# An attention LSTM in a decoder: wait order, place of an output gate product, sums, alphas and cell order inside one time step

## The chip, the cores and the metric

The kernel runs on one core of a Trainium2 chip, in float32. The metric is the device time of one execution in microseconds. The median of three executions of the kernel before is 5745.92 us (5745.6 to 5747.82). A stretch of 512 dependent time steps of an LSTM with attention takes most of it.

## The reference, cut to what matters

The program is a two-layer decoder over x of shape (4, 512, 256). All five edits lie in the second block of the first layer, an LSTM (hidden size 256) whose input at each step contains the attention output of the step before. For a batch of 4 and 512 steps, in short:

```
for t in range(512):
    gates = x[t] @ W_x + attn @ W_attn + h @ W_hid + b      # i, f, g, o: 1024 columns
    c = sigmoid(f) * c + sigmoid(i) * tanh(g)
    h = sigmoid(o) * tanh(c)
    alpha = softmax((h @ Wq) . context)                      # over 512 source positions
    attn = tanh([alpha @ context, h] @ Wout)
    x[t] += attn
```

Each step needs the one before it whole, so its latency counts 512 times.

## The kernel before, in words

Everything of the step lies on chip. The keys already hold Wq and the values already hold the context part of Wout. Sigmoids are computed as tanh of half the argument. TensorE's array is used as four quarters (QUARTERS = 4): a product such as `gate_sums`, `scores` or `context` is issued as instructions to the four quarters that run side by side, and a float32 matmul appears in the trace as two weight loads and two matmuls. So one call of `scores(c, k)`, `context(c, n)`, `half_attn(c, k)` or `half_hid(c, k)` is eight loads and eight matmuls.

The hidden state, the cell and the gates i, f, g are kept in two halves k = 0, 1 of the hidden units. `gates` (L892 on) computes the next step's gates: `o_gate_x_hid` (the o gate's x part and both hidden parts, 64 columns each), `half_attn` four times (96 columns each; it waits for `attn_ready[0]` and before its second call for `attn_ready[1]`), then `o_gate_attn`. VectorE transposes each half (`turn_half`, L1011), ScalarE takes its tanh (L978) and the o gate's (L982, between the two halves), VectorE makes the products and the new cell (`cell_products` L1016, `new_cell` L1022), transposes the o gate (L1046), ScalarE takes tanh of the cell (L986), and `new_hidden` (L1029) gives half of h. TensorE multiplies h with the keys: `scores(c, k)` for four source chunks c; with half 0 of h chunks 0 and 1 can start, and then `h_ready[1]` is needed.

The softmax is done in two parts of two chunks each: VectorE takes the negated maximum (L1053), ScalarE the exponential (L989), TensorE turns the result with `turn(part)` (L882), and it is copied to `alpha` (part 0 on ScalarE, L993; part 1 on VectorE, L1063). `context(c, n)` (L873) adds chunk c into three column pieces n of 128, 64 and 64. Beside it VectorE and ScalarE work out the scale of the parts (`lstm_shrink` L995, `lstm_own_terms` L1068, ... `lstm_sel_scaled` L1080), the three pieces are copied to `out_row` (L998, L1000 on ScalarE, L1083 on VectorE), `select(o)` (L890) forms the attention row and ScalarE's tanh (L1004) gives `attn`. GpSimd adds it to x (L1097) and signals `attn_kept`.

Every engine runs its list in the order written; what sets the order is that list and the `wait_ge` calls in it. The DMA queue of SyncE loads one row of x parts a step (L795); no edit touches it.

The lines touched: L840 to L847 (o gate), L939 to L947 (turn and context), L986 to L1004 (ScalarE), L1047 to L1067 (VectorE).

Of the kernel before, what the change touches and what calls it, by code (L numbers as in the profile page):

```python
# [17 lines left out]
KC = DIM // P  # L18
# [644 lines left out]
def attention_lstm_phase(nc, d, g):  # L663
# [14 lines left out]
    with Scope(nc) as s:  # L678
# [14 lines left out]
        with Scope(nc) as q:  # L693
# [57 lines left out]
            first_total_ready = q.sem("lstm_first_total_ready")  # L751
# [33 lines left out]
            def alpha_rows(part):  # L785
                return alpha[:, :, 2 * part:2 * part + 2, SPACE - 1]
# [22 lines left out]
            def _(pe):  # L809
# [3 lines left out]
                def gate_sums(ps, cols, rows, w, start=False, stop=False):  # L813

                    for j in range(QUARTERS):
                        mm = pe.matmul(ps[j * STRIP:j * STRIP + ROWS, :], rows, w[:, j * HID + cols.start:j * HID + cols.stop],  # L816
                                       start=start, stop=stop)
                    return mm
# [17 lines left out]

                def o_gate_x_hid(u):

                    gate_sums(o_gate_ps, o_cols, place, xg[:, u, :], start=True).then_inc(xg_used, 1)
                    for c in range(KC):  # L840
                        gate_sums(o_gate_ps, o_cols, hid[:, c, PAD:PAD + ROWS], w_hid[:, c, :])

                def o_gate_attn():

                    for c in range(KC):
                        mm = gate_sums(o_gate_ps, o_cols, attn[:, c, 0:ROWS], w_attn[:, c, :], stop=c == KC - 1)
                    mm.then_inc(o_ready, 1)  # L847
# [70 lines left out]
                with pe.Fori(0, SEQ // UNROLL) as i:  # L918
                    for u in range(UNROLL):
# [17 lines left out]
                        for n in range(PIECES):  # L937
                            context(0, n)
                        pe.wait_ge(exp_ready, 2 * t + 2)  # L939
                        turn(1)  # L940
                        for n in range(PIECES):
                            context(1, n)
# [22 lines left out]
            def _(act):  # L965
# [4 lines left out]
                with act.Fori(0, SEQ // UNROLL) as i:  # L970
                    for u in range(UNROLL):
# [15 lines left out]
                        for part in range(PARTS):  # L987
                            act.wait_ge(max_ready, 2 * t + part + 1)
                            act.activation(expo[:, part, :], score_ps[part], ACT.Exp, bias=neg_max[:, part:part + 1],  # L989
                                           accum_out=total[:, 1:PARTS] if part == 1 else None).then_inc(exp_ready, 1)  # L990
                            if part == 0:
                                act.wait_ge(alpha_turned, 2 * t + 1)
                                act.copy(alpha_rows(0), turned_rows(0)).then_inc(alpha_ready[0], 1)  # L993
# [7 lines left out]
                        act.wait_ge(attn_kept, t + 1)  # L1001
                        for o in range(KC):
                            act.wait_ge(attn_summed[o], t + 1)
                            act.activation(by_batch(attn[:, o, :]), attn_ps[o], ACT.Tanh).then_inc(attn_ready[o], 1)  # L1004

            @block.vector
            def _(dve):
# [30 lines left out]
                with dve.Fori(0, SEQ // UNROLL) as i:  # L1038
                    for u in range(UNROLL):
# [7 lines left out]
                        cell_products(t, 1)  # L1047
                        new_hidden(t, 0)
                        new_cell(t, 1)
# [10 lines left out]
                        dve.wait_ge(exp_ready, 2 * t + 1)  # L1060
                        dve.tensor_reduce(total[:, 0:1], expo[:, 0, :], AX_X, ALU.add).then_inc(first_total_ready, 1)
                        dve.wait_ge(alpha_turned, 2 * t + 2)
                        dve.tensor_copy(alpha_rows(1), turned_rows(1)).then_inc(alpha_ready[1], 1)  # L1063
                        dve.wait_ge(first_total_ready, t + 1)
                        dve.wait_ge(exp_ready, 2 * t + 2)
                        dve.transpose(spread_blocks(spread_total[:, :]), every_row(total[:, :])).then_inc(total_spread, 1)
# [1578 lines left out]
```

## Time and profile before

| | us |
|---|---|
| median of the three runs | 5745.92 |
| the profiled execution's own time | 5744.19 |
| its span in the profile | 5742.4 |
| first to last tanh wait of the 512 steps (511 periods) | 195.4 to 3934.0 |

Outside this loop lie the preparation (the first 190 us) and the second half of the decoder (after 3934 us), which the change leaves alone. The trace gives instructions with start and length in us on each engine; PE is TensorE's matmuls, PEld its weight loads, DVE VectorE, ACT ScalarE, POOL GpSimd; a row with xN merges N neighbouring instructions, with its length from the first start to the last end. In brackets stands the idle time of the engine before it and what ended it.

### The profile page before, as it was taken

Reading aid. Unit: us, or ns where it says so; the run is one execution under the profiler, and the core shown is the slowest. Engines: PE = TensorE matmul, PEld = TensorE weight load, DVE = VectorE, ACT = ScalarE, POOL = GpSimd, SP = SyncE. Lnnn points to the kernel's source line nnn. Section 1 sums busy time; section 2 is a strip of 40 time slices with the busy share of each in tenths; the row PEclk is TensorE's granted clock in tenths of the full one; section 3 lists DMA queues with packets and bytes.
Section 4 is the critical chain, followed back from the end, with each engine's and each line's share of the span. In section 5 each row is a group of like instructions: output and inputs, shape, how many; then the busy total and the mean of one; then the engine's idle time right before and its main releaser. Section 6 shows DMA issues by size and latency. Waiting matters only on the chain. (4 is left out here: it accounts for less than half of the span.)

```text
span 5742.4 us, 383675 instructions
## 1 busy us (share of the span) xinstructions
PE 5219.3 (91%) x171240; PEld 3816.0 (66%) x171240; DVE 3449.3 (60%) x15922; ACT 1998.5 (35%) x7977; POOL 350.1 (6%) x795
## 2 busy tenths in 40 slices
PE   9899999999999999999999999998688879797989
PEld 4677777777777777777777777776444434343433
DVE  5455555555555555555555555554798999999931
ACT  2244444444444444444444444442222222223221
POOL 0000000000000000000000000000121211212100
PEclk9999999999999999999999999999799889898999
DMA  2000000000000000000000000002111101010111
GB/s 99 35 2 2 2 2 2 2 2 2 2 2 2 2 2 2 2 2 2 2 2 2 2 2 2 2 2 81 50 52 41 42 18 54 25 54 25 56 37 54
DMA packets 45677, 111.60 MB, mean 19 GB/s; under 512 B 8192, under 2 KB 10240, under 8 KB 45072
## 3 DMA queue, kind: packets, MB, share of 16 engines
q1 hardware_dynamic: 44144, 109.39, 6.2%
q10 hardware_dynamic: 1440, 1.06, 0.1%
q8 instruction: 48, 0.79, 0.1%
q14 instruction: 45, 0.37, 0.0%
HBM read 99.90 MB, written 10.52 MB: 19 GB/s over the span
## 5 line engine op out<-in xcount | busy, mean ns | idle before, releaser
L857 PE MATMUL lstm_part_ps<-lstm_keys,lstm_hid 128*4 128x128 f32 x32768 | 1024.9, 273 | 207.0 <-DVE lstm_hid L1029 207.0
L857 PEld LDWEIGHTS lstm_part_ps<-lstm_keys,lstm_hid 128*4 128x4 f32 x32768 | 771.1, 86 | 430.0 <-DVE lstm_hid L1029 416.2
L873 PE MATMUL lstm_ctx_ps<-lstm_values,lstm_alpha 128*4 128x128 f32 (+1 forms) x49152 | 1051.7, 237 | 0.5 <-issue 0.5
L873 PEld LDWEIGHTS lstm_ctx_ps<-lstm_values,lstm_alpha 128*4 128x4 f32 x49152 | 903.0, 86 | 89.4 <-issue 0.7
L1053 DVE TENSOR_REDUCE lstm_neg_max<-lstm_part_ps 128x1 f32<-128x128 f32 x1024 | 299.1, 292 | 679.0 <-PE lstm_part_ps L857 679.0
L1011 DVE STREAM_TRANSPOSE lstm_gates<-lstm_half_ps 128x96 f32<-128x96 f32 x1026 | 290.6, 283 | 567.7 <-PE lstm_half_ps L816 543.8
L989 ACT ACTIVATE lstm_expo<-lstm_part_ps,lstm_neg_max 128x128 f32<-128x128 f32 x1024 | 376.3, 367 | 648.5 <-DVE lstm_neg_max L1053 648.5
L816 PE MATMUL lstm_half_ps<-lstm_w_hid,lstm_hid 128*13 128x96 f32 x16384 | 563.8, 245 | 0.0
L816 PE MATMUL lstm_half_ps<-lstm_w_attn,lstm_attn 128*13 128x96 f32 x16448 | 434.8, 246 | 1.3 <-issue 1.3
L2090 ACT ACTIVATE mix_gated<-mix_gate_ps 115x512 f32<-115x512 f32 (+2 forms) x200 | 112.6, 563 | 777.7 <-PE mix_gate_ps L1818 772.8
L978 ACT ACTIVATE lstm_cell<-lstm_gates 128x12 f32<-128x12 f32 x1024 | 224.8, 220 | 411.1 <-DVE lstm_gates L1011 411.1
L816 PEld LDWEIGHTS lstm_half_ps<-lstm_w_hid,lstm_hid 128*13 128x13 f32 x16384 | 367.3, 94 | 0.0
L1818 PE MATMUL mix_gate_ps<-xT,mix_ring 128*115 128x512 f32 (+3 forms) x800 | 364.3, 579 | 0.0
L1827 PE MATMUL mix_up_ps<-mix_xw,mix_ring 128*115 128x512 f32 (+2 forms) x704 | 320.5, 579 | 44.9 <-DVE mix_weighted L2394 36.9
L1847 PE MATMUL mix_down_ps<-mix_weighted,mix_ring 115*128 115x512 f32 (+3 forms) x800 | 358.1, 571 | 0.8 <-DVE mix_weighted L2394 0.7
L1097 POOL TENSOR_TENSOR xT<-xT,lstm_attn 128x8 f32 x512 | 105.2, 206 | 3645.9 <-ACT lstm_attn L1004 3645.9
L816 PEld LDWEIGHTS lstm_half_ps<-lstm_w_attn,lstm_attn 128*13 128x13 f32 x16448 | 302.9, 93 | 19.0 <-issue 1.7
L816 PE MATMUL lstm_half_ps<-lstm_xg,lstm_masks 128*13 128x96 f32 x8224 | 306.8, 250 | 8.6 <-DMA lstm_xg<-xg_rows 8.6
L998 ACT COPY lstm_out_row<-lstm_ctx_ps 128x128 f32<-128x128 f32 x512 | 136.4, 266 | 508.4 <-PE lstm_ctx_ps L873 508.4
L2367 DVE TENSOR_TENSOR rw_terms<-rw_state,rw_sc 128x384 f32<-128x384 f32 x512 | 297.5, 581 | 6.7
L986 ACT ACTIVATE lstm_tanh_c<-lstm_cell 128x4 f32<-128x4 f32 x1024 | 210.3, 205 | 196.0 <-DVE lstm_cell L1022 154.2
L1029 DVE SCALAR_TENSOR_TENSOR lstm_hid<-lstm_o_col,lstm_tanh_c 128x4 f32<-128x4 f32 x1024 | 170.5, 167 | 173.9 <-ACT lstm_tanh_c L986 139.0
(326 smaller groups left out, 8236.0 us busy)
## 6 DMA issues: line engine op xcount, KB each, us to landing
mix_ring<-in_sm_chunks SPq DMA_DIRECT2D x120, 358.0 KB, 2.9
mix_ring<-in_mix_chunks SPq DMA_DIRECT2D x80, 384.0 KB, 3.0
lstm_xg<-xg_rows SPq DMA_DIRECT2D x514, 16.0 KB
xg_rows<-rec_lam SPq DMA_DIRECT2D x16, 512.0 KB, 2.6
xT<-in_xT SPq DMA_DIRECT2D x4, 512.0 KB, 8.4
ctxT<-in_ctxT SPq DMA_DIRECT2D x1, 2048.0 KB, 14.1
out_xT<-xT SPq DMA_DIRECT2D x4, 512.0 KB, 3.8
lstm_w_x<-in_lstm_w_x SPq DMA_DIRECT2D x1, 1024.0 KB, 17.4
```

Of the source, the lines that this page charges most:

```text
L816: mm = pe.matmul(ps[j * STRIP:j * STRIP + ROWS, :], rows, w[:, j * HID + cols.start:j * HID + cols.stop], start=start, stop=stop)
L857: mm = pe.matmul(part_rows(score_ps[part], b), hid[:, k, lo:lo + SPACE], keys[:, k, b * SRC + c * P:b * SRC + (c + 1) * P], start=(n == 0 ...
L873: mm = pe.matmul(part_rows(ctx_ps[n], b), alpha[:, b, c, SPACE - 1 - c:2 * SPACE - 1 - c], values[:, b * SC + c, ctx_cols[n]], start=(c == ...
L978: act.activation(cell[:, k, 0:GATES - 1, :], by_batch(turned), ACT.Tanh).then_inc(half_tanh[k], 1)
L986: act.activation(tanh_c[:, k, :], cell[:, k, GATES - 1, :], ACT.Tanh, scale=0.5).then_inc(c_tanh[k], 1)
L989: act.activation(expo[:, part, :], score_ps[part], ACT.Exp, bias=neg_max[:, part:part + 1], accum_out=total[:, 1:PARTS] if part == 1 else ...
L1011: dve.transpose(gates[:, k, :], half_ps[k]).then_inc(half_turned[k], 1)
L1053: dve.tensor_reduce(neg_max[:, part:part + 1], score_ps[part], AX_X, ALU.max, negate=True)\
L1818: mm = pe.matmul(gate_ps[0:m, 0:width], ring[:, at, k * e:k * e + m], token_block(x, i)[:, k, :], start=(k == 0), stop=(k == KC - 1))
L1827: mm = pe.matmul(up_ps[0:m, 0:width], ring[:, at, lo:lo + m], xw[:, k, 0:width] if x.weighted(n) else token_block(x, i)[:, k, :], start=(k ...
L1847: mm = pe.matmul(down_ps[:, o_, 0:width], ring[0:m, gn % RING, lo + o_ * P:lo + (o_ + 1) * P], gw[0:m, gn % 2, 0:width], start=(n == 0), s ...
L2367: dve.tensor_tensor(terms[:, :, :, :], before.unsqueeze(1).to_broadcast([P, 3, HALF, HD]), sc[:, parity, UNIT_KEY:RECV + 1, t, :].unsqueez ...
```

## The change

Five edits inside one time step:

1. ScalarE, attention's tanh: the wait on `attn_kept` is written behind the wait on `attn_summed[0]`, no longer ahead of the loop.
2. TensorE, o gate: the product of half 1 of h with the o gate's weights moves from before the four `half_attn` calls to after them.
3. Sums: both parts' sums of exponentials are one VectorE reduction over 2x128; before, part 0's was a VectorE reduction and part 1's came with the exponential from ScalarE's accumulator.
4. Alphas: part 1's copy to `alpha` moves from VectorE to ScalarE, directly behind its exponential; on TensorE `turn(1)` moves ahead of the last piece of `context(0, n)`.
5. VectorE, cell: `new_cell(t, 1)` moves ahead of `new_hidden(t, 0)`.

```diff
@@ o gate @@
+                def o_gate_hid(c):
+                    gate_sums(o_gate_ps, o_cols, hid[:, c, PAD:PAD + ROWS], w_hid[:, c, :])
+
                 def o_gate_x_hid(u):
                     gate_sums(o_gate_ps, o_cols, place, xg[:, u, :], start=True).then_inc(xg_used, 1)
-                    for c in range(KC):
-                        gate_sums(o_gate_ps, o_cols, hid[:, c, PAD:PAD + ROWS], w_hid[:, c, :])
+                    o_gate_hid(0)

                 def o_gate_attn():
+                    o_gate_hid(1)
                     for c in range(KC):
                         mm = gate_sums(o_gate_ps, o_cols, attn[:, c, 0:ROWS], w_attn[:, c, :], stop=c == KC - 1)
@@ tensor @@
                         pe.wait_ge(alpha_ready[0], t + 1)
-                        for n in range(PIECES):
+                        for n in range(PIECES - 1):
                             context(0, n)
                         pe.wait_ge(exp_ready, 2 * t + 2)
                         turn(1)
+                        context(0, PIECES - 1)
                         for n in range(PIECES):
                             context(1, n)
@@ scalar @@
                         for part in range(PARTS):
                             act.wait_ge(max_ready, 2 * t + part + 1)
-                            act.activation(expo[:, part, :], score_ps[part], ACT.Exp, bias=neg_max[:, part:part + 1],
-                                           accum_out=total[:, 1:PARTS] if part == 1 else None).then_inc(exp_ready, 1)
-                            if part == 0:
-                                act.wait_ge(alpha_turned, 2 * t + 1)
-                                act.copy(alpha_rows(0), turned_rows(0)).then_inc(alpha_ready[0], 1)
+                            act.activation(expo[:, part, :], score_ps[part], ACT.Exp,
+                                           bias=neg_max[:, part:part + 1]).then_inc(exp_ready, 1)
+                            act.wait_ge(alpha_turned, 2 * t + part + 1)
+                            act.copy(alpha_rows(part), turned_rows(part)).then_inc(alpha_ready[part], 1)
...
-                        act.wait_ge(attn_kept, t + 1)
                         for o in range(KC):
                             act.wait_ge(attn_summed[o], t + 1)
+                            if o == 0:
+                                act.wait_ge(attn_kept, t + 1)
                             act.activation(by_batch(attn[:, o, :]), attn_ps[o], ACT.Tanh).then_inc(attn_ready[o], 1)
@@ vector @@
                         cell_products(t, 1)
+                        new_cell(t, 1)
                         new_hidden(t, 0)
-                        new_cell(t, 1)
                         new_hidden(t, 1)
...
-                        dve.wait_ge(exp_ready, 2 * t + 1)
-                        dve.tensor_reduce(total[:, 0:1], expo[:, 0, :], AX_X, ALU.add).then_inc(first_total_ready, 1)
-                        dve.wait_ge(alpha_turned, 2 * t + 2)
-                        dve.tensor_copy(alpha_rows(1), turned_rows(1)).then_inc(alpha_ready[1], 1)
-                        dve.wait_ge(first_total_ready, t + 1)
                         dve.wait_ge(exp_ready, 2 * t + 2)
+                        dve.tensor_reduce(total[:, :], expo[:, :, :], AX_X, ALU.add).then_inc(totals_ready, 1)
+                        dve.wait_ge(totals_ready, t + 1)
                         dve.transpose(spread_blocks(spread_total[:, :]), every_row(total[:, :])).then_inc(total_spread, 1)
```

## Rows read from the trace of the kernel before

**Rows 1.** One stretch: length, busy us (count) of PE, PEld, DVE, ACT, POOL; PEclk, DMA.
```profile
1300.00:2300.00 1000.00, 944.58 (x44343) 793.89 (x44339) 523.73 (x3286) 411.67 (x1916) 28.14 (x137) 1.00 0.01 2
```
**Rows 2.** One source line: duration in ns min/median/max, first and last start.
```profile
L1003 ACTq EVENT_SEMAPHORE  x512: 17/17/17, 195.4 to 3934.0; - x171
```
**Rows 3.** Timeline, attention row to the gates: start, length, instruction, count.
```profile
2011.61 0.34 ACT L1004 ACTIVATE lstm_attn<-lstm_part_ps 128x4 f32<-128x4 f32 x2 [0.47 <-PE lstm_part_ps L890]
2011.85 0.84 PE L816 MATMUL lstm_half_ps<-lstm_w_attn,lstm_attn 128*13 128x96 f32 x32
2012.43 0.31 PEld L816 LDWEIGHTS lstm_ctx_ps<-lstm_w_attn,lstm_attn 128*13 128x13 f32 x16
```
**Rows 4.** Timeline of weight loads alone, a narrow window: the call that needs attention's second half.
```profile
2012.00 0.13 PEld L816 LDWEIGHTS lstm_half_ps<-lstm_w_attn,lstm_attn 128*13 128x13 f32 x8
```
**Rows 5.** Timeline, gates to the hidden state and the first scores.
```profile
2012.98 0.22 ACT L982 ACTIVATE lstm_o_row<-lstm_ctx_ps 128x64 f32<-128x64 f32 x1
2013.10 0.22 ACT L978 ACTIVATE lstm_cell<-lstm_gates 128x12 f32<-128x12 f32 x1
2013.20 0.16 DVE L1022 SCALAR_TENSOR_TENSOR lstm_cell<-lstm_uv 128x4 f32<-128x4 f32 x1
2013.29 0.24 DVE L1046 STREAM_TRANSPOSE lstm_o_col<-lstm_o_row 128x64 f32<-128x64 f32 x1
2013.45 0.12 DVE L1016 SCALAR_TENSOR_TENSOR lstm_uv<-lstm_cell 128x8 f32<-128x8 f32 x1
2013.64 0.17 DVE L1029 SCALAR_TENSOR_TENSOR lstm_hid<-lstm_o_col,lstm_tanh_c 128x4 f32<-128x4 f32 x1
2013.72 0.16 DVE L1022 SCALAR_TENSOR_TENSOR lstm_cell<-lstm_uv 128x4 f32<-128x4 f32 x1
2013.86 0.33 PEld L857 LDWEIGHTS lstm_part_ps<-lstm_keys,lstm_hid 128*4 128x4 f32 x16 [0.64 <-DVE lstm_hid L1029]
2014.14 0.17 DVE L1029 SCALAR_TENSOR_TENSOR lstm_hid<-lstm_o_col,lstm_tanh_c 128x4 f32<-128x4 f32 x1 [0.27 <-ACT lstm_tanh_c L986]
2014.37 0.11 PEld L857 LDWEIGHTS lstm_part_ps<-lstm_keys,lstm_hid 128*4 128x4 f32 x8 [0.18 <-DVE lstm_hid L1029]
```
**Rows 6.** Timeline of the step before, the same view: all scores behind the second half of h.
```profile
2007.05 1.20 PEld L857 LDWEIGHTS lstm_part_ps<-lstm_keys,lstm_hid 128*4 128x4 f32 x48 [0.18 <-DVE lstm_hid L1029]
```
**Rows 7.** Timeline, alphas and context.
```profile
2016.26 0.37 ACT L989 ACTIVATE lstm_expo<-lstm_part_ps,lstm_neg_max 128x128 f32<-128x128 f32 x1
2016.34 0.44 PEld L873 LDWEIGHTS lstm_ctx_ps<-lstm_values,lstm_alpha 128*4 128x4 f32 x24
2016.52 0.19 ACT L989 ACTIVATION_READ_ACCUMULATOR lstm_expo<-lstm_part_ps,lstm_neg_max 128x1 f32 x1
2016.61 0.28 DVE L1061 TENSOR_REDUCE lstm_total<-lstm_expo 128x1 f32<-128x128 f32 x1
2016.73 0.30 ACT L995 ACTIVATE lstm_shrink<-lstm_spread_max,lstm_neg_max_all 128x4 f32<-128x4 f32 x1
2016.76 0.16 PEld L882 LDWEIGHTS lstm_part_ps<-lstm_ident,lstm_expo 128*32 128x32 f32 x8
2017.10 0.17 DVE L1063 COPY lstm_alpha<-lstm_part_ps 128x8 f32<-128x8 f32 x1 [0.22 <-PE lstm_part_ps L882]
2017.35 0.12 DVE L1068 SCALAR_TENSOR_TENSOR lstm_own_terms<-lstm_shrink,lstm_masks 128x4 f32<-128x4 f32 x1
2017.89 0.22 DVE L1080 SCALAR_TENSOR_TENSOR lstm_sel_scaled<-lstm_sel_shrunk,lstm_inverse,lstm_masks 128x4 f32<-128x4 f32 x1
2018.46 0.21 PEld L890 LDWEIGHTS lstm_part_ps<-lstm_sel_scaled,lstm_out_row 128*32 128x32 f32 x8
```
**Rows 8.** Timeline of weight loads alone, two narrow windows: before and at the alpha wait.
```profile
2017.12 0.16 PEld L873 LDWEIGHTS lstm_ctx_ps<-lstm_values,lstm_alpha 128*4 128x4 f32 x8
...
2017.33 0.11 PEld L873 LDWEIGHTS lstm_ctx_ps<-lstm_values,lstm_alpha 128*4 128x4 f32 x8
```

More of the change, by code:

```diff
@@ L750, in attention_lstm_phase @@
             shrink_ready = q.sem("lstm_shrink_ready")
-            first_total_ready = q.sem("lstm_first_total_ready")
+            totals_ready = q.sem("lstm_totals_ready")
             total_spread = q.sem("lstm_total_spread")
```

## The prediction

> **What bounds the kernel now.** I read the stretches first: in the loop TensorE is busy 94% of the time at a granted clock of 1.00 [rows 1], so the clock is at its upper level and no edit changes what it does enough to move it. Then the loop's period: the wait in front of attention's tanh stands 512 times between 195.4 and 3934.0 us, 511 periods of 7.316 us [rows 2]. The timelines of one step then show that it is one ring, part latency, part TensorE's own work. The reader should look for the places where TensorE stands with an empty list: before the first score (0.64 us for the loads) and again at the second half of h (0.18) [rows 5], and at part 1's alphas (below) [rows 8]. Between these TensorE works through its list without a hole, and there only its own length counts. So each edit is priced at the next place where TensorE has to wait. 0.2% of the time, about what a measurement can tell from no change, is 11.5 us or 0.0225 us a step.
>
> **TensorE's own pace.** The 48 score loads behind the second h half span 1.20 us [rows 6]; twelve groups of four, the first two issued together, each load 0.09 long: (1.20 - 0.09)/10 = 0.11 per four, 0.22 per call. Two calls of 64 columns span 0.31 - 0.09 = 0.22 from first to last load [rows 3], 0.11 per call. Four calls of 96 columns take 0.84 for 32 matmuls of 0.25 [rows 3]: near 0.165 a call with the rounding and a short wait.
>
> **Edit 1, wait order.** The trace has a separate record for the wait on `attn_summed[0]` (line 1003) in every step [rows 2], and none that belongs to the wait on `attn_kept`. So of two waits the one written last becomes an instruction of its own, ahead of the one that carries the first; today that is the late one. After the change it is `attn_kept`, signalled by GpSimd long before. The gain at the first tanh lies between 0 and 0.16, its distance from the second [rows 3]; I take 0.06, as the record and the step behind it can hardly cost more. Nothing hangs on its size, as the next paragraph shows. The Trainium skill says the same of the mechanism ("Perfetto Trace Analysis", section "Identifying Dependency Chains": waits on several engines may be put into EventSemaphore instructions ahead); it gives no price, and none of it enters the sum.
>
> **Edit 2, o gate.** Today TensorE starts `half_attn(0, 0)` at 2011.85; the first tanh ended at 2011.61 + 0.18 = 2011.79, and with the 0.05 that a signal takes to TensorE (exponential's end to `turn(1)`, below) this start is bound by the tanh and by TensorE's own list at once, as near as the rows can tell [rows 3]. With one call of 0.11 moved away and the tanh 0.06 earlier, `half_attn(0, 0)` starts near 2011.79. But the next call needs the second tanh, which ends at 2011.61 + 0.34 = 2011.95 and waits for its own product, so edit 1 does not move it; its loads stand at 2012.00 [rows 4], just where the previous call's 0.165 ends (2011.85 + 0.165 = 2012.01). So the first gates gain 0.01 us only (0 to 0.014), and that is all that edits 1 and 2 give. The price: the moved 0.11 now stands in front of `o_gate_attn`. `o_ready` comes 0.11 - 0.01 = 0.10 later. I follow that through [rows 5]: the o tanh was at 2012.98 and goes to 2013.08, ending 2013.30. The second gate tanh is queued behind it on ScalarE, 0.12 later as now: 2013.20 to 2013.42. VectorE's transpose of o stood at 2013.29, 0.09 behind the new cell though its input was ready at 2013.20 + 0.035; so 0.05 of the delay is absorbed and it goes to 2013.34. `cell_products(1)` follows 0.16 behind: 2013.50 to 2013.62 (now 2013.45).
>
> **Edit 5, second cell first.** The second new cell starts 0.03 behind its product: 2013.65 instead of 2013.72. The first h half is now queued behind it, 0.08 later as the pair stands today (2013.64, 2013.72): 2013.73 to 2013.74 instead of 2013.64, so 0.10 late. From the second new cell over its tanh to the second half of h is 0.42 (2013.72, 2014.14): it comes at 2014.08 instead of 2014.14, 0.06 early. TensorE's loads come 0.22 behind each. The first scores start at 2013.96; two calls of 0.22 must run before the second h half is used: 2014.40. The second h half would allow 2014.30. The later one counts: 2014.40 against 2014.37 now. The wait for the second h half disappears, and the first one takes its place. Sum: +0.035 us a step (+0.02 to +0.05 by the rounding of six steps).
>
> A rule that speaks against this edit: the Trainium skill, "VectorE: DVE Perf Modes", section "The DRAIN you can't avoid", says that the next VectorE instruction does not start until the pipe is empty. By that the first half of h would wait for the whole new cell. The pair of the first h half and the second new cell disagrees: 0.08 between starts, with an instruction 0.17 long in front [rows 5]. The measurement decides; by the page the outcome would be rival C below.
>
> **Edits 3 and 4, sums and alphas.** All times here in [rows 7, 8]. The exponential of part 1 ends at 2016.63, but its signal comes with the accumulator read, at 2016.71, and `turn(1)` starts 0.05 later, 2016.76. Its copy is at 2017.10 to 2017.27, and `context(2, 0)` loads at 2017.33. The last call before it began its loads at 2017.12; two fours of 0.055 put its successor's load at 2017.23 and matmul at 2017.29. TensorE loses 0.04 us there. After the change the signal comes at 2016.63, and TensorE has done the first two pieces at 2016.34 + 0.22 + 0.11 = 2016.67, so `turn(1)` starts near 2016.68, with at most 0.01 of wait. The copy, now on ScalarE, comes 0.31 to 0.34 later and lasts 0.17 to 0.18: done by 2017.20, usable at 2017.25, before 2017.29. TensorE no longer waits. Gain 0.04 us (0.02 to 0.045); it can't be more, since TensorE's own calls fill the time from 2016.34 on.
>
> Behind that, `lstm_shrink` is queued behind the copy: latest 2017.20 + 0.04, 0.30 long, 2017.54. The one VectorE reduction over 2x128 columns takes between 0.28 and twice that, so it ends by 2016.66 + 0.56 = 2017.22, and its transpose before the scale needs it: it is not last. `lstm_own_terms` then starts at 2017.57 instead of 2017.35, the scale is done 0.76 later at 2018.33, usable 2018.38; `select(0)` loads at 2018.46 - 0.04 = 2018.42. It is hidden by 0.04 at worst and 0.2 if `lstm_shrink` takes the 0.2 of the other small activations. Without that cover each further 0.01 would cost 5 us. I cost it at nothing.
>
> **The sum.** +0.035 - 0.04 = -0.005 us a step, times 512 = -2.6 us. The profiled execution (5744.19) would be 5741.6; the median is 1.7 above it, so 5743.3. With the bounds (0.02 - 0.045 and 0.05 - 0.02, so -0.025 to +0.03) it is 5733 to 5761.
>
> **The rivals.**
> *A, faster: the first h half does not hold the scores.* If it were not late at all, the first scores would start at 2013.86 as today and the second half's at 2013.86 + 0.44 = 2014.30, where the second h half also comes: 0.07 early, with the alphas' 0.04 a gain of 0.11, 5688. If it is half as late as I count, 0.05, the start is 2014.35: 0.02 + 0.04 = 0.06 a step, 31 us, 5713. For it: the o gate's path had 0.05 of slack, and VectorE's or ScalarE's queue may have more than I see. Against: transpose, product, cell and h are four instructions in one queue, and each distance is measured. I take 5713.
>
> *B, slower: the alphas still come last.* If the copy on ScalarE is usable after 2017.29, the 0.04 is not gained and the 0.035 stands alone: +18 us, 5764. It decides from 0.04 us more than I count between `turn(1)` and the alphas. Against it: part 0 takes this very path today.
>
> *C, slower: VectorE finishes the new cell before h starts.* The new cell is 0.16 long [rows 5], so the first h half would stand 0.16 instead of 0.08 behind its start: +0.08 more, +0.075 in all, +38 us, 5784. Against it stands today's pair with its 0.08. This is what the Trainium skill's page above, "VectorE: DVE Perf Modes", section "The DRAIN you can't avoid", would make of it.
>
> *D, the change does nothing that counts*: the compiler keeps the waits as they are, edit 1 is void. As edit 2 hangs on the second tanh, this only moves 0.01 and stays within my forecast.
>
> **How the numbers follow.** Forecast (with D) 0.63, A 0.19, B 0.12, C 0.06. The time is the forecast's, 5743.3. The forecast's own range 5733 to 5761 holds 0.6; the range I give reaches to A's middle and to B: 5712 to 5765. Faster by over 0.2%: A and a little of the forecast's lower edge, 0.2; slower: B, C and a little, 0.18; within: 0.62.
>
> **What would show it.** Right: no idle time in front of the second group of scores and about 0.10 more in front of the first; `turn(1)` near 0.33 behind the first context load and no hole before `context(2, 0)`; the o tanh 0.10 later against the first gate tanh; the first h half 0.08 behind the second cell. Wrong: a wait for the second h half still there with an earlier start (A), a hole at part 1's alphas (B), or `select(0)` waiting for `lstm_sel_scaled` (an unpriced loss).

## The result, and the profile after

| | before | after |
|---|---|---|
| median, us (17 runs each) | 5744.86 (5743.66 to 5747.82) | 5756.6 (5754.38 to 5760.27) |
| span of the profiled execution | 5742.4 | 5754.8 |

The ratio is 1.0022, with a 95% interval of 1.0015 to 1.0028: the changed kernel is 11.7 us slower. The forecast was 5743.3, a gain of 0.005 us a step; 11.7 / 512 is a loss of 0.023 us a step. So 0.028 us a step are to be explained.

First, where it is. The line that forms h runs twice a step; its first and last start bound the loop. Source line views, before, then after, with the separate wait record at attention's tanh:

```profile
L1029 DVE SCALAR_TENSOR_TENSOR lstm_hid<-lstm_o_col,lstm_tanh_c x1024: 165/166/168, 189.5 to 3929.3; 128x4 f32<-128x4 f32 x171
```
```profile
L1034 DVE SCALAR_TENSOR_TENSOR lstm_hid<-lstm_o_col,lstm_tanh_c x1024: 164/166/168, 189.0 to 3939.9; 128x4 f32<-128x4 f32 x171
...
L1008 ACTq EVENT_SEMAPHORE  x512: 17/17/17, 194.2 to 3944.1; - x171
```

The loop takes 3739.8 before and 3750.9 after: 11.1 of the span's 12.4 us lie in it. The clock did not move [rows 1]; the same stretch in the kernel after:

```profile
1300.00:2300.00 1000.00, 928.78 (x44186) 804.21 (x44177) 559.48 (x3134) 403.78 (x1907) 27.78 (x136) 1.00 0.01 2
```

Next, the stage in which the hidden state is made, to be held against [rows 5]. Timeline of one step after (start, length, instruction, idle time before it):

```profile
2009.87 0.22 ACT L983 ACTIVATE lstm_cell<-lstm_gates 128x12 f32<-128x12 f32 x1 [0.79 <-DVE lstm_gates L1016]
2010.22 0.22 ACT L987 ACTIVATE lstm_o_row<-lstm_ctx_ps 128x64 f32<-128x64 f32 x1
...
2010.34 0.22 ACT L983 ACTIVATE lstm_cell<-lstm_gates 128x12 f32<-128x12 f32 x1
2010.47 0.24 DVE L1051 STREAM_TRANSPOSE lstm_o_col<-lstm_o_row 128x64 f32<-128x64 f32 x1
...
2010.64 0.12 DVE L1021 SCALAR_TENSOR_TENSOR lstm_uv<-lstm_cell 128x8 f32<-128x8 f32 x1
2010.80 0.16 DVE L1027 SCALAR_TENSOR_TENSOR lstm_cell<-lstm_uv 128x4 f32<-128x4 f32 x1
2010.88 0.17 DVE L1034 SCALAR_TENSOR_TENSOR lstm_hid<-lstm_o_col,lstm_tanh_c 128x4 f32<-128x4 f32 x1
2011.10 0.77 PEld L861 LDWEIGHTS lstm_part_ps<-lstm_keys,lstm_hid 128*4 128x4 f32 x32 [0.75 <-DVE lstm_hid L1034]
...
2011.23 0.17 DVE L1034 SCALAR_TENSOR_TENSOR lstm_hid<-lstm_o_col,lstm_tanh_c 128x4 f32<-128x4 f32 x1 [0.19 <-ACT lstm_tanh_c L991]
```

The o gate's tanh now starts 0.35 behind the first gate tanh and still 0.12 ahead of the second, and TensorE waits 0.75 us in front of its first score where it waited 0.64. The second group of scores has no bracket any more: 32 loads run on in one row where [rows 5] shows 16, then a wait of 0.18. The page's groups show the same over all 512 steps: the loads' wait for h falls from 416.2 to 386.4 us and the matmuls' wait rises from 207.0 to 268.0 us. The loads run ahead of the matmuls, so the matmuls' row is the one that counts for the first half of h: its 61 us more are 0.12 a step. It does not show the matmuls' stall in front of the second half, which was there before and is gone; the medians below have it. Groups of the page, before, then after (busy, mean ns, idle before them):

```profile
L857 PE MATMUL lstm_part_ps<-lstm_keys,lstm_hid 128*4 128x128 f32 x32768 | 1024.9, 273 | 207.0 <-DVE lstm_hid L1029 207.0
L857 PEld LDWEIGHTS lstm_part_ps<-lstm_keys,lstm_hid 128*4 128x4 f32 x32768 | 771.1, 86 | 430.0 <-DVE lstm_hid L1029 416.2
...
L873 PEld LDWEIGHTS lstm_ctx_ps<-lstm_values,lstm_alpha 128*4 128x4 f32 x49152 | 903.0, 86 | 89.4 <-issue 0.7
```
```profile
L861 PE MATMUL lstm_part_ps<-lstm_keys,lstm_hid 128*4 128x128 f32 x32768 | 988.3, 273 | 268.0 <-DVE lstm_hid L1034 268.0
L861 PEld LDWEIGHTS lstm_part_ps<-lstm_keys,lstm_hid 128*4 128x4 f32 x32768 | 811.4, 86 | 414.1 <-DVE lstm_hid L1034 386.4
...
L877 PEld LDWEIGHTS lstm_ctx_ps<-lstm_values,lstm_alpha 128*4 128x4 f32 x49152 | 905.9, 86 | 64.0 <-issue 0.6
```

Last, the alphas, to be held against [rows 7, 8]. Timeline after:

```profile
2013.42 0.37 ACT L994 ACTIVATE lstm_expo<-lstm_part_ps,lstm_neg_max 128x128 f32<-128x128 f32 x1
2013.51 0.33 PEld L877 LDWEIGHTS lstm_ctx_ps<-lstm_values,lstm_alpha 128*4 128x4 f32 x16
2013.83 0.42 DVE L1066 TENSOR_REDUCE lstm_total<-lstm_expo 128x2 f32<-128x256 f32 x1
2013.84 0.16 PEld L886 LDWEIGHTS lstm_part_ps<-lstm_ident,lstm_expo 128*32 128x32 f32 x8
2013.85 0.25 PE L886 MATMUL lstm_part_ps<-lstm_ident,lstm_expo 128*32 128x8 f32 x8
2013.90 1.01 PEld L877 LDWEIGHTS lstm_ctx_ps<-lstm_values,lstm_alpha 128*4 128x4 f32 x52
2013.93 1.17 PE L877 MATMUL lstm_ctx_ps<-lstm_values,lstm_alpha 128*4 128x64 f32 x48
2014.16 0.17 ACT L997 COPY lstm_alpha<-lstm_part_ps 128x8 f32<-128x8 f32 x1 [0.37 <-PE lstm_part_ps L886]
2014.22 0.30 ACT L999 ACTIVATE lstm_shrink<-lstm_spread_max,lstm_neg_max_all 128x4 f32<-128x4 f32 x1
2014.56 0.16 DVE L1070 SCALAR_TENSOR_TENSOR lstm_own_terms<-lstm_shrink,lstm_masks 128x4 f32<-128x4 f32 x1
```

`turn(1)` stands 0.33 behind the first context load, and behind it 52 loads run on without a hole: the wait before `context(2, 0)` is gone. A single step's rows are rounded to a hundredth of a us, so for finer sizes I took the medians of 480 steps in the middle of each trace. The step's period (from one start of h's first half to the next) is 7.310 by them before and 7.333 after. From the first score of h's first half to the first of the second half, TensorE's matmuls took 0.505 before and take 0.437 now. From the first matmul of `context(1, 0)` to the first of `context(2, 0)`, the stretch with the hole of [rows 8], it was 0.479 and is 0.440: the hole of 0.04 is gone.

### The profile page after: what moved, and what is told of

Same layout as the page of the kernel before. It is cut to its first block and busy times, and to the rows that moved or that the text cites. A ratio compares the mean times of both kernels' runs of the same rounds, so it can differ in the third digit from the quotient of the medians.

```text
span 5754.8 us, 382651 instructions
## 1 busy us (share of the span) xinstructions
PE 5170.2 (90%) x171240; PEld 3860.8 (67%) x171240; DVE 3594.2 (62%) x15410; ACT 1976.1 (34%) x7977; POOL 344.6 (6%) x795
## 5 line engine op out<-in xcount | busy, mean ns | idle before, releaser
L861 PE MATMUL lstm_part_ps<-lstm_keys,lstm_hid 128*4 128x128 f32 x32768 | 988.3, 273 | 268.0 <-DVE lstm_hid L1034 268.0
L861 PEld LDWEIGHTS lstm_part_ps<-lstm_keys,lstm_hid 128*4 128x4 f32 x32768 | 811.4, 86 | 414.1 <-DVE lstm_hid L1034 386.4
L816 PE MATMUL lstm_half_ps<-lstm_w_attn,lstm_attn 128*13 128x96 f32 x16448 | 467.4, 248 | 1.0 <-issue 1.0
L997 ACT COPY lstm_alpha<-lstm_part_ps 128x8 f32<-128x8 f32 x1024 | 176.8, 173 | 377.2 <-PE lstm_part_ps L886 377.2
L816 PE MATMUL lstm_ctx_ps<-lstm_w_hid,lstm_hid 128*13 128x64 f32 x8208 | 302.1, 219 | 0.0
L1849 PEld LDWEIGHTS mix_down_ps<-mix_weighted,mix_ring 115*128 115x128 f32 (+2 forms) x800 | 149.6, 192 | 185.1 <-issue 164.2
```

Source lines behind the costliest of these rows:

```text
L861: mm = pe.matmul(part_rows(score_ps[part], b), hid[:, k, lo:lo + SPACE], keys[:, k, b * SRC + c * P:b * SRC + (c + 1) * P], start=(n == 0 ...
L997: act.copy(alpha_rows(part), turned_rows(part)).then_inc(alpha_ready[part], 1)
L1849: mm = pe.matmul(down_ps[:, o_, 0:width], ring[0:m, gn % RING, lo + o_ * P:lo + (o_ + 1) * P], gw[0:m, gn % 2, 0:width], start=(n == 0), s ...
```

## The experiments

In the table "step" is that median period. Each kernel's ratio is to its own runs of the kernel before. These came in three groups, with medians of 5744.05 (x12, x5, x34_alphas_sums, x1345_o_gate_back), 5743.39 (x1, x2, x1234, x1345_turn_in_middle) and 5744.82 (the other four), so a difference between kernels of different groups is good to some 1.5 us only.

| kernel | edits | us | ratio, 95% interval | step |
|---|---|---|---|---|
| x1_wait_order | 1 | 5742.28 | 0.9997 [0.9988, 1.0006] | 7.304 |
| x2_o_gate | 2 | 5774.59 | 1.0054 [1.0040, 1.0068] | 7.367 |
| x12_wait_and_o_gate | 1, 2 | 5774.60 | 1.0054 [1.0040, 1.0068] | 7.367 |
| x5_cell_first | 5 | 5730.35 | 0.9977 [0.9967, 0.9986] | 7.283 |
| x34_alphas_sums | 3, 4 | 5734.64 | 0.9985 [0.9976, 0.9994] | 7.287 |
| x125_no_alphas | 1, 2, 5 | 5767.80 | 1.0042 [1.0028, 1.0056] | 7.355 |
| x1234_second_h_first | 1 to 4 | 5762.56 | 1.0033 [1.0021, 1.0045] | 7.344 |
| x1345_o_gate_back | 1, 3, 4, 5 | 5723.57 | 0.9964 [0.9950, 0.9977] | 7.267 |
| x34_turn_stays | 3, 4, no move of `turn(1)` | 5744.38 | 1.0002 [0.9993, 1.0011] | 7.308 |
| x4_keep_accumulator | 4 | 5781.81 | 1.0067 [1.0053, 1.0080] | 7.383 |
| x1345_turn_stays | 1, 3, 4, 5, no move of `turn(1)` | 5732.08 | 0.9977 [0.9968, 0.9986] | 7.283 |
| x1345_turn_in_middle | 1, 3, 4, 5, `turn(1)` between | 5716.95 | 0.9955 [0.9941, 0.9968] | 7.254 |

**Which edit loses.** Theory: edit 2, whose delay of the o gate edit 5 only partly makes good. Rivals: edit 5, by holding back the first half of h, and edits 3 and 4. The first three runs do one part of the change each, on the kernel before.

Edits 1 and 2 alone:

```diff
+                def o_gate_hid(c):
+                    gate_sums(o_gate_ps, o_cols, hid[:, c, PAD:PAD + ROWS], w_hid[:, c, :])
...
                 def o_gate_x_hid(u):
                     gate_sums(o_gate_ps, o_cols, place, xg[:, u, :], start=True).then_inc(xg_used, 1)
-                    for c in range(KC):
-                        gate_sums(o_gate_ps, o_cols, hid[:, c, PAD:PAD + ROWS], w_hid[:, c, :])
+                    o_gate_hid(0)
...
                 def o_gate_attn():
+                    o_gate_hid(1)
...
-                        act.wait_ge(attn_kept, t + 1)
                         for o in range(KC):
                             act.wait_ge(attn_summed[o], t + 1)
+                            if o == 0:
+                                act.wait_ge(attn_kept, t + 1)
```

> The kernel before with edits 1 and 2 alone (wait order at attention's tanh, o gate product of the second half of h behind the attention products). Theory (the loss sits in edit 2: the o gate's tanh comes 0.10 us later and VectorE's queue behind it shifts): without the second cell moved ahead, the first half of h starts 0.07 us later and the second half too, so +0.07 us a step, +36 us: about 5781. Rival 1 (the loss comes from the second cell ahead of the first h, edit 5): 0 to -7 us, 5738 to 5745. Rival 2 (the loss comes from the alphas and sums, edits 3 and 4): the same, 5738 to 5745.

Measured: 5774.6, 30.5 us slower, 6 less than expected. The sign and most of the size are right. Timeline of VectorE in this kernel:

```profile
2011.76 0.24 DVE L1051 STREAM_TRANSPOSE lstm_o_col<-lstm_o_row 128x64 f32<-128x64 f32 x1
2011.93 0.12 DVE L1021 SCALAR_TENSOR_TENSOR lstm_uv<-lstm_cell 128x8 f32<-128x8 f32 x1
2012.11 0.17 DVE L1034 SCALAR_TENSOR_TENSOR lstm_hid<-lstm_o_col,lstm_tanh_c 128x4 f32<-128x4 f32 x1
2012.19 0.15 DVE L1027 SCALAR_TENSOR_TENSOR lstm_cell<-lstm_uv 128x4 f32<-128x4 f32 x1
2012.61 0.17 DVE L1034 SCALAR_TENSOR_TENSOR lstm_hid<-lstm_o_col,lstm_tanh_c 128x4 f32<-128x4 f32 x1 [0.27 <-ACT lstm_tanh_c L990]
```

The product follows the transpose in VectorE's list, so the late o gate holds up the second cell too; that is how the second half of h comes late in this kernel.

Edit 5 alone:

```diff
                         cell_products(t, 1)
+                        new_cell(t, 1)
                         new_hidden(t, 0)
-                        new_cell(t, 1)
                         new_hidden(t, 1)
```

> The kernel before with edit 5 alone (second new cell ahead of the first half of h). Theory: the second cell starts 0.11 us earlier, the first half of h 0.05 later; TensorE then has two calls of scores from the first half before it can use the second one, which leaves -0.023 us a step: -12 us, about 5733. Rival 1 (edit 5 is the loss): +0.04 us a step or more, 5765 and above. Rival 2: as the theory.

Measured: 5730.35, 13.7 us faster; the rival falls. Timeline of VectorE:

```profile
2007.22 0.12 DVE L1016 SCALAR_TENSOR_TENSOR lstm_uv<-lstm_cell 128x8 f32<-128x8 f32 x1
2007.38 0.16 DVE L1022 SCALAR_TENSOR_TENSOR lstm_cell<-lstm_uv 128x4 f32<-128x4 f32 x1
2007.46 0.17 DVE L1029 SCALAR_TENSOR_TENSOR lstm_hid<-lstm_o_col,lstm_tanh_c 128x4 f32<-128x4 f32 x1
2007.81 0.17 DVE L1029 SCALAR_TENSOR_TENSOR lstm_hid<-lstm_o_col,lstm_tanh_c 128x4 f32<-128x4 f32 x1 [0.19 <-ACT lstm_tanh_c L986]
```

Before, h's first half stood 0.19 behind the product [rows 5], held by the first cell's tanh, with VectorE idle. The second cell now fills that gap, and h's first half stands 0.24 behind the product: it pays 0.046 by the medians (0.238 against 0.192), while the scores of the second half start 0.656 behind it instead of 0.726. Less 0.070 and more 0.046 make -0.024 a step; the period fell by 0.027.

Edits 3 and 4 alone:

```diff
-                        for n in range(PIECES):
+                        for n in range(PIECES - 1):
                             context(0, n)
                         pe.wait_ge(exp_ready, 2 * t + 2)
                         turn(1)
+                        context(0, PIECES - 1)
...
-                                           accum_out=total[:, 1:PARTS] if part == 1 else None).then_inc(exp_ready, 1)
...
+                            act.copy(alpha_rows(part), turned_rows(part)).then_inc(alpha_ready[part], 1)
...
+                        dve.tensor_reduce(total[:, :], expo[:, :, :], AX_X, ALU.add).then_inc(totals_ready, 1)
```

> The kernel before with edits 3 and 4 alone (one VectorE reduction for both sums, both alpha copies on ScalarE, part 1's turn one piece earlier). Theory: the hole before the third chunk of context goes (0.04 us), but the turn now starts from an idle TensorE with its weight loads in the open (0.02), so -0.02 us a step: -10 us, about 5735. Rival 1: the same. Rival 2 (these edits are the loss): +0.02 us a step or more, 5755 and above.

Measured: 5734.64, 9.4 us faster, where the forecast's 0.04 a step would have made 20.

The changed kernel with the o gate as before:

```diff
                 def o_gate_x_hid(u):
                     gate_sums(o_gate_ps, o_cols, place, xg[:, u, :], start=True).then_inc(xg_used, 1)
-                    o_gate_hid(0)
+                    for c in range(KC):
+                        gate_sums(o_gate_ps, o_cols, hid[:, c, PAD:PAD + ROWS], w_hid[:, c, :])
...
                 def o_gate_attn():
-                    o_gate_hid(1)
```

> The changed kernel with edit 2 undone (both hidden products of the o gate ahead of the attention products, as before), edits 1, 3, 4 and 5 kept. Theory: -0.023 and -0.02 us a step add, -0.043 in all: -22 us, about 5723, faster than both kernels. Rival 1 (edit 5 is the loss): 5750 or above. Rival 2 (alphas and sums are the loss): 5745 to 5755.

Measured: 5723.57, 20.5 us below its own runs of the kernel before, where the changed kernel was 11.7 above: undoing edit 2 gives 32 us. Edits 1 and 2 cost 30.5 on the kernel before, and edit 2 by itself, below, 31.2. It is the whole of the loss and more, and both rivals fall.

**Does edit 1 pay for edit 2?** Edit 1 alone moves one line, edit 2 alone moves the o gate's product; their diffs are the two halves of the first one above:

```diff
-                        act.wait_ge(attn_kept, t + 1)
                         for o in range(KC):
                             act.wait_ge(attn_summed[o], t + 1)
+                            if o == 0:
+                                act.wait_ge(attn_kept, t + 1)
```

> The kernel before with edit 1 alone. Theory: the first half of attn is ready about 0.09 us earlier, but TensorE is still at the o gate's products then, so nothing moves: 5744 (within 2 us). Rival (the late wait as an instruction of its own costs on the path): -0.05 us a step or more, 5720.

```diff
-                    for c in range(KC):
-                        gate_sums(o_gate_ps, o_cols, hid[:, c, PAD:PAD + ROWS], w_hid[:, c, :])
+                    o_gate_hid(0)
...
                 def o_gate_attn():
+                    o_gate_hid(1)
```

> The kernel before with edit 2 alone. Theory: as with edits 1 and 2 together, where 5774.6 was measured, since edit 1 only moves a start that the second half of attn bounds anyway: 5775 to 5779. Rival (edit 1 is what pays for edit 2): 5790 or above.

Measured: 5742.28, no difference that can be told from zero, and 5774.59. With edit 1 added it is 5774.60, and the step is 7.367 in both. So the earlier first tanh is worth nothing that these runs can tell (the step of edit 1 alone is 0.006 shorter, 3 us).

**What edit 5 is worth beside the others.** The changed kernel with the cells in their old order:

```diff
                         cell_products(t, 1)
-                        new_cell(t, 1)
                         new_hidden(t, 0)
+                        new_cell(t, 1)
```

> The changed kernel with edit 5 undone (first half of h ahead of the second cell, as before). Theory: 5774.6 of edits 1 and 2 less the 9.4 us of edits 3 and 4: 5765, slower than the changed kernel (5756.6), so edit 5 helps there too. Rival (edit 5 holds the first half of h and costs): faster than 5756, near 5745.

Measured: 5762.56. Edit 5 gives about 6 us here (5762.6 - 5756.6; 0.011 a step, 5.6 us, by the medians) and 13.7 alone. With the o gate late, the product comes late, and h's first half stands only 0.18 behind it (x12_wait_and_o_gate) where it stood 0.192 before: the first cell's tanh starts 0.30 ahead of h there, against 0.24 before, so it no longer holds h, and less of the gap is left for the second cell to fill. With the cell ahead it is 0.24 in both. So edit 5 costs the first half 0.06 here and 0.05 alone, against the same 0.07 won.

**Where the alphas' gain went.** The changed kernel without edits 3 and 4:

```diff
-                        for n in range(PIECES - 1):
+                        for n in range(PIECES):
                             context(0, n)
                         pe.wait_ge(exp_ready, 2 * t + 2)
                         turn(1)
-                        context(0, PIECES - 1)
```

with the sums and the copy as before too (not shown).

> The changed kernel with edits 3 and 4 undone: edits 1, 2 and 5 alone. Theory: the changed kernel (+12) plus the 9.4 us that edits 3 and 4 give: +21 us, about 5765. Rival (edits 3 and 4 cost in this combination, since the select's scale comes later): 5750 or below.

Measured: 5767.8, so edits 3 and 4 give 11 us in the full change too, 0.022 a step.

The next run goes back to the kernel before. It has edits 3 and 4, but with `turn(1)` left behind `context(0, n)` (the sums as in edit 3, not shown):

```diff
                         for n in range(PIECES):
                             context(0, n)
                         pe.wait_ge(exp_ready, 2 * t + 2)
                         turn(1)
...
+                            act.copy(alpha_rows(part), turned_rows(part)).then_inc(alpha_ready[part], 1)
```

> Edits 3 and 4 without the move of part 1's turn: the turn stands behind all of context(0, n) as before; one reduction on VectorE, both alpha copies on ScalarE. Theory: the turn starts no earlier than before (TensorE is busy until then), but its loads are hidden, and ScalarE starts the copy 0.02 us sooner behind the turn than VectorE does (0.242 against 0.264 from the turn's last matmul in the traces); the third chunk waits 0.02 less: 5734 to 5737, as much as with the move. Rival (the move is what gains): 5744.

Measured: 5744.38, the rival's number; my expectation of a gain fell. Timeline of this kernel, loads and ScalarE:

```profile
2007.39 0.44 PEld L873 LDWEIGHTS lstm_ctx_ps<-lstm_values,lstm_alpha 128*4 128x4 f32 x24
2007.78 0.18 PEld L882 LDWEIGHTS lstm_part_ps<-lstm_ident,lstm_expo 128*32 128x32 f32 x8
...
2008.15 0.17 ACT L992 COPY lstm_alpha<-lstm_part_ps 128x8 f32<-128x8 f32 x1 [0.48 <-PE lstm_part_ps L882]
```

The turn's loads start as soon as TensorE's list lets them, 0.39 behind the first context load against 0.42 [rows 7]. But its first matmul stands 0.442 behind the first context matmul in both kernels, and the copy still starts 0.76 behind that load, just as VectorE's did (2016.34 to 2017.10). Queued behind streaming products, the turn's last matmul starts 0.261 to 0.269 before the copy; started from a wait, 0.242 to 0.244. I had put that difference down to VectorE and ScalarE. This run has the longer one on ScalarE, and the kernel before on VectorE, so it belongs to how the turn starts and not to the engine. Counted from the turn's first matmul it is the same, 0.315 to 0.318, in all these kernels.

Edit 4 with the accumulator kept, that is, without edit 3:

```diff
-                        for n in range(PIECES):
+                        for n in range(PIECES - 1):
                             context(0, n)
                         pe.wait_ge(exp_ready, 2 * t + 2)
                         turn(1)
+                        context(0, PIECES - 1)
...
                             act.activation(expo[:, part, :], score_ps[part], ACT.Exp, bias=neg_max[:, part:part + 1],
                                            accum_out=total[:, 1:PARTS] if part == 1 else None).then_inc(exp_ready, 1)
-                            if part == 0:
-                                act.wait_ge(alpha_turned, 2 * t + 1)
-                                act.copy(alpha_rows(0), turned_rows(0)).then_inc(alpha_ready[0], 1)
+                            act.wait_ge(alpha_turned, 2 * t + part + 1)
+                            act.copy(alpha_rows(part), turned_rows(part)).then_inc(alpha_ready[part], 1)
...
-                        dve.wait_ge(alpha_turned, 2 * t + 2)
-                        dve.tensor_copy(alpha_rows(1), turned_rows(1)).then_inc(alpha_ready[1], 1)
```

> Edit 4 alone: both alpha copies on ScalarE and the turn one piece earlier, while part 1's sum still comes with ScalarE's accumulator and part 0's from VectorE. Theory: the signal behind the exponential still comes with the accumulator's read, 0.09 us behind the end of the exponential; the turn, now needed one piece earlier, waits for it with TensorE empty: +0.07 us a step against before, +36 us: about 5780. Rival (dropping the accumulator is without effect): 5735.

Measured: 5781.81, 37 us slower than the kernel before and 46 slower than with edit 3 added. Timeline, loads and ScalarE:

```profile
2004.92 0.33 PEld L873 LDWEIGHTS lstm_ctx_ps<-lstm_values,lstm_alpha 128*4 128x4 f32 x16
2005.35 0.16 PEld L882 LDWEIGHTS lstm_part_ps<-lstm_ident,lstm_expo 128*32 128x32 f32 x8
...
2004.84 0.37 ACT L990 ACTIVATE lstm_expo<-lstm_part_ps,lstm_neg_max 128x128 f32<-128x128 f32 x1
2005.10 0.19 ACT L990 ACTIVATION_READ_ACCUMULATOR lstm_expo<-lstm_part_ps,lstm_neg_max 128x1 f32 x1
```

The signal comes with the accumulator read, and the turn stands 0.424 behind the first context load instead of 0.333 (medians): TensorE has nothing in its list for that 0.09, and 0.09 times 512 is the 46 us. So edits 3 and 4 are one edit: the move of the turn pays only when the signal is early, and the early signal pays only when the turn is moved.

The same question on the kernel without edit 2, the turn left in its old place:

```diff
-                        for n in range(PIECES - 1):
+                        for n in range(PIECES):
                             context(0, n)
                         pe.wait_ge(exp_ready, 2 * t + 2)
                         turn(1)
-                        context(0, PIECES - 1)
```

> Edits 1, 3, 4 and 5 with part 1's turn behind all of context(0, n) as before. Theory: the gains of edit 5 (13.7 us) and of edits 3 and 4 without the move add up: 5720 to 5724, the same as with the move (5723.6) and behind the turn in the middle of the piece (5717). Rival (the move gains on its own): 5730.

Measured: 5732.08, again near the rival's number. It is some 8 us above the kernel in which the turn is moved (0.016 a step by the medians).

**A better place for the turn.** If the turn loses by starting from an empty list, half of the last piece ahead of it should cover it. This run has edits 1, 3, 4 and 5 (the kernel without edit 2); the diff shows TensorE's part against the kernel before:

```diff
-                def context(c, n):
+                def context(c, n, batches=range(BATCH)):
...
-                    for b in range(BATCH):
+                    for b in batches:
...
-                        for n in range(PIECES):
+                        for n in range(PIECES - 1):
                             context(0, n)
+                        context(0, PIECES - 1, range(0, BATCH // 2))
                         pe.wait_ge(exp_ready, 2 * t + 2)
                         turn(1)
+                        context(0, PIECES - 1, range(BATCH // 2, BATCH))
```

> Edits 1, 3, 4 and 5, with part 1's turn in the middle of the last piece of context(0, n): two of its four batches before, two after. Theory (the turn's weight loads stand in the open when it starts from an idle TensorE, 0.02 us): the wait is over when TensorE gets to the turn, the loads are hidden, and the alphas still come in time: up to -0.02 us a step against edits 1, 3, 4 and 5 (5723.6), 5713 to 5716. Rival (the turn costs the same wherever it stands, or half a piece fills the array worse): 5723 to 5740.

Measured: 5716.95, 26 us below the kernel before and so 38 below the changed one, the fastest of all; about 6 us better than with the turn ahead of the whole piece (6.7 by the step). Timeline of its loads:

```profile
2010.15 0.43 PEld L873 LDWEIGHTS lstm_ctx_ps<-lstm_values,lstm_alpha 128*4 128x4 f32 x20
2010.49 0.16 PEld L882 LDWEIGHTS lstm_part_ps<-lstm_ident,lstm_expo 128*32 128x32 f32 x6
2010.55 0.12 PEld L873 LDWEIGHTS lstm_ctx_ps<-lstm_values,lstm_alpha 128*4 128x4 f32 x4
2010.59 0.12 PEld L882 LDWEIGHTS lstm_part_ps<-lstm_ident,lstm_expo 128*32 128x32 f32 x2
2010.62 0.82 PEld L873 LDWEIGHTS lstm_ctx_ps<-lstm_values,lstm_alpha 128*4 128x4 f32 x40
```

Loads of the turn and of context are mixed in time. By the medians `context(2, 0)` starts 0.960 behind the first context matmul, against 0.968 with the turn ahead of the whole piece, and 0.227 behind the copy, just as in the kernel before (0.228): here the alphas come last again, but earlier. Of the 0.013 a step that this kernel is faster, 0.006 to 0.008 lies ahead of `select(0)`. The rest lies between the second gate tanh and h. No edit between the two kernels touches that stretch, and from the first gate tanh to h it is 0.936 to 0.941 in the four kernels with edit 5 and without edit 2: the rest is no larger than that spread, and its cause stays open. The half piece, batches 0 and 1, covers two of the four quarters only; other splits were not tried.

## Why the prediction was wrong

The time lay inside the range given, but on the other side of no change than the forecast. No rival happened: the mechanisms are those of the forecast, and two of its terms were mis-sized, each still within its own bounds (+0.02 to +0.05, and 0.02 to 0.045).

**What bounds the kernel, edit 1, no clock effect: right.** The wait that is a record of its own is now the one on `attn_kept`, one per step. The first tanh comes earlier, the second doesn't, and the second bounds the gates. Both tanh instructions together now span 0.40 instead of 0.34 [rows 3], the start 0.06 earlier that I took:

```profile
2016.01 0.40 ACT L1009 ACTIVATE lstm_attn<-lstm_part_ps 128x4 f32<-128x4 f32 x2 [0.41 <-PE lstm_part_ps L894]
```

**Edits 2 and 5: right in kind, +0.045 instead of +0.035 a step.** Counted from the first gate tanh, the o tanh comes 0.112 later (x125_no_alphas against before), as worked out: 0.10, with the gates 0.01 earlier. From there the queue on VectorE takes a little more than I read off rows rounded to 0.01: it absorbs 0.045 of the delay where I had 0.05, the product stands 0.169 behind the transpose instead of 0.16, and the cell 0.159 behind the product where I had 0.15. The first half of h comes 0.120 later by that count, and I had 0.11. The other side was right: the scores of h's second half start 0.069 earlier behind h's first half (I had 0.07), and the gates gained 0.006 where I had taken 0.01. The sum is 0.120 - 0.069 - 0.006 = 0.045, the period of x125_no_alphas less that of before.

**Edits 3 and 4: right in kind, -0.023 instead of -0.040 a step.** This is the step that failed: "TensorE no longer waits. Gain 0.04 us". The hole did go. The stretch that held it fell by 0.039, as forecast (0.479 to 0.440). But I costed `turn(1)` at the same length in its new place. Before, it was queued behind 24 loads of context, and its weight loads were in hand while the products in front still streamed: its first load starts 0.021 ahead of its first matmul, and from that to the next call's matmul it is 0.065 us. In its new place its load starts 0.052 behind the exponential's end, the time the signal takes, just when TensorE's list has run empty; its first load starts only 0.002 ahead of its first matmul, and the distance to the next call's is 0.084. Timeline of matmuls before, to be held against 2013.85 and 2013.93 above:

```profile
2016.78 0.23 PE L882 MATMUL lstm_part_ps<-lstm_ident,lstm_expo 128*32 128x8 f32 x8
2016.85 0.89 PE L873 MATMUL lstm_ctx_ps<-lstm_values,lstm_alpha 128*4 128x128 f32 x32
```

From the first context matmul to the first of `context(2, 0)` it was 0.987 before, I had 0.947, and it is 0.968. I had even written "at most 0.01 of wait" for that place; what I did not ask is what a call costs that starts from a wait, although the trace before shows a turn in both conditions: part 0's starts from a wait and takes the same 0.084 to the next call. The runs bear this out: the distance is 0.084 wherever the moved turn starts from a wait (with edits 3 and 4 alone, and in x4_keep_accumulator) and 0.060 to 0.068 wherever it is queued. With half a piece in front of the turn the whole stretch is 0.960 (x1345_turn_in_middle). Part of the 6 us of the latter is open, as told above.

**The sum.** +0.045 - 0.023 = +0.022 a step, 11.3 us of the 11.7 measured. Both errors, 0.010 and 0.017, have the same sign, and each is larger than the 0.005 that the two halves of my sum left, so the sign of the forecast was within its own error.

**The scale behind the alphas: right.** `lstm_own_terms` starts at 2014.56; the scale is done 0.77 later, near 2015.33, and `select(0)` loads 0.28 behind that. From `context(2, 0)` to `select(0)` it is 1.213 after and 1.214 before, so the scale is still hidden. Timeline after, weight loads:

```profile
2015.61 0.21 PEld L894 LDWEIGHTS lstm_part_ps<-lstm_sel_scaled,lstm_out_row 128*32 128x32 f32 x8
```

**The rivals.** A did not happen: the first half of h does hold the scores. B did not: there is no hole at the alphas, though half of the gain that it denied is missing for another reason. C fell on the row of the cell and h, 2010.80 and 2010.88: h starts 0.08 behind a cell that is 0.16 long. The Trainium skill ("VectorE: DVE Perf Modes", section "The DRAIN you can't avoid") says that the next instruction does not start until the pipe is empty, by which h would wait for the whole cell. The same section adds that a next instruction which is not held starts earlier, and the prediction left that out; the 0.08 here agrees with the second sentence and not with the first alone. D did not happen: the waits changed places. The prices of A (5688 and 5713) were added to the profiled execution and lack the 1.7 us that B, C and the forecast have; it changes nothing.

## What to carry to other kernels

Where an edit's sum is the small difference of two terms, take each from many steps and not from a timeline's rounded rows: errors of 0.01 and 0.02 us a step decided the sign here. An edit that only moves work past a wait has its price at the next queue: the o gate's product gave nothing where it left, since the second tanh bounded that place, and cost 0.06 us a step where it went. Ask of a short call whether it will start from an empty list: here that made it 0.02 us longer, and the kernel with half a piece left in front of it was the fastest, though only part of its gain is traced to that.

## What the runs showed of the hardware

- The turn (a float32 product of eight loads and eight matmuls) is dearer when it starts from a wait than when it is queued: 0.084 against 0.060 to 0.068 us from its first matmul to its successor's. Its consumer starts 0.315 to 0.318 behind its first matmul either way, on VectorE and ScalarE alike.
- With the turn in the middle of a piece, the four matmuls of a group, one to a quarter, start in two pairs about 0.036 us apart for a while, where in the other kernels they start within 0.021 of each other: two quarters run ahead of the other two (6 turn loads, then 4 of context, then 2 of the turn, in the rows above). So the quarters are not in lockstep. Whether that has a part in the 6 us was not tried.
